# Attention with group normalisation: VectorE's order in slot 0, at the turn of a chunk, and the third chunk's scores over two chunks

## The reference

```
n = groupnorm(x), 32 groups
f = Wq n, g = Wk n (64 x 4096 each), h = Wv n (256 x 4096)
scores[n, m] = sum_q f[q, n] g[q, m]          (4096 x 4096 for each image)
beta = softmax over n of scores
out = x + (gamma * (h beta) + groupnorm(x))
```

## Time and profile before

| | us |
|---|---|
| median of 3 runs | 1918.55 (1916.56 to 1918.79) |
| the profiled execution | 1918.76 |
| its span, first to last instruction | 1917.0 |
| TensorE matmuls busy | 1886.6 |
| VectorE busy | 1631.2 |
| ScalarE busy | 1578.0 |
| GpSimd busy | 1307.8 |

### The profile page before, as it was taken

How to read it: one execution, slowest core, us unless ns; L and a number is a source line. 1 busy time by engine, 2 the same in 40 slices (tenths; PEclk the granted TensorE clock), 3 DMA queues, 4 the chain that set the end, 5 groups by cost and what they waited for, 6 DMA issues and landing times. The chain is left out here.

```text
span 1917.0 us, 44195 instructions
## 1 busy us (share of the span) xinstructions
PE 1886.6 (98%) x17369; PEld 1555.9 (81%) x17369; DVE 1631.2 (85%) x2238; ACT 1578.0 (82%) x1677; POOL 1307.8 (68%) x757
## 2 busy tenths in 40 slices
PE   7899999999999999999999999999999999999999
PEld 4678888877888888887888888888788888888888
DVE  7889998987879999888877999998787788888885
ACT  4788888988768888987877888899787788888885
POOL 4367668876556776886664766788665577767777
PEclk9999999999999999999999999999999999999999
DMA  4022212212102221211211221122121111111111
GB/s 144 4 67 57 67 31 59 66 30 52 44 21 73 75 56 23 76 53 23 70 37 40 53 70 53 37 65 53 29 65 31 22 32 34 24 33 31 33 32 37
DMA packets 200111, 91.19 MB, mean 48 GB/s; under 512 B 150240, under 2 KB 191712, under 8 KB 199904
## 3 DMA queue, kind: packets, MB, share of 16 engines
q1 hardware_dynamic: 199904, 88.36, 17.8%
HBM read 46.60 MB, written 16.78 MB: 33 GB/s over the span
## 5 line engine op out<-in xcount | busy, mean ns | idle before, releaser
L390 POOL TENSOR_TENSOR PL<-SC,PH 128x1024 f16<-128x1024 f32 x511 | 1092.2, 2143 | 549.9 <-ACT SC L643 544.4
L505 PE MATMUL O<-V,PH 128*128 128x257 f16 x4096 | 1119.1, 273 | 0.1
L507 PE MATMUL O<-V,PL 128*128 128x257 f16 x4096 | 1118.8, 273 | 0.0
L506 PE MATMUL O<-V,PH 128*128 128x256 f16 x4096 | 1117.3, 273 | 0.0
L636 ACT ACTIVATE SC<-S 128x1024 f32<-128x1024 f32 x512 | 504.1, 1013 | 136.8 <-issue 122.7
L884 DVE TENSOR_TENSOR SC<-SC,MB 128x1024 f32<-128x1024 f32 x511 | 613.6, 1211 | 0.1
L642 ACT ACTIVATE PH<-SC 128x1024 f16<-128x1024 f32 x511 | 539.4, 1056 | 84.0 <-PE O L507 62.7
L643 ACT ACTIVATE SC<-SC 128x1024 f32<-128x1024 f32 x511 | 532.8, 1043 | 0.0
L841 DVE TENSOR_TENSOR XM<-S,XM 128x1024 f32<-128x1024 f32 x384 | 468.6, 1220 | 74.4 <-PE S L493 64.7
L506 PEld LDWEIGHTS O<-V,PH 128*128 128x128 f16 x4096 | 401.1, 98 | 51.0
L507 PEld LDWEIGHTS O<-V,PL 128*128 128x128 f16 x4096 | 401.1, 98 | 50.1
(11 more groups left out here) (117 smaller groups left out, 1029.4 us busy)
## 6 DMA issues: line engine op xcount, KB each, us to landing
xin<-x SPq DMA_DIRECT2D x24, 1024.0 KB, 5.6
xres<-x SPq DMA_DIRECT2D x64, 256.0 KB, 3.0
ATT<-OT SPq DMA_DIRECT2D x1008, 16.0 KB, 1.8
out<-RES SPq DMA_DIRECT2D x63, 256.0 KB, 2.2
SC<-x SPq DMA_DIRECT2D x8, 512.0 KB, 7.1
F<-GG SPq DMA_DIRECT2D x64, 64.0 KB, 2.0
GG<-GG SPq DMA_DIRECT2D x32, 128.0 KB, 2.4
SC<-wvT SPq DMA_DIRECT2D x1, 256.0 KB, 7.1
```

The source lines that it names most:

```text
L390: pool.tensor_tensor(PL[:, s % RING, :], sc(s), PH[:, s % RING, :], ALU.subtract).then_inc(pl_ready, 1)
L505: mm(o[:, 0:C + 1], PH[:, n % RING, cols], vh, start=t == 0, stop=False)
L506: mm(o[:, 0:C], PH[:, n % RING, cols], vl, start=False, stop=False)
L507: w = mm(o[:, 0:C + 1], PL[:, n % RING, cols], vh, start=False, stop=t == T - 1)
```

## The change

It has three parts.

1. Slot 0. VectorE's maximum(9) moves from between the two halves of slot 0's subtraction to ahead of column_maxima(0). ScalarE's store(9) moves from behind the exponentials of slot 0's first half to ahead of them. (The exchange in the change's name is the sequence of quadrant_maxima, column_maxima and spread_maxima.)
2. The turn of a chunk. Where g is 0 and k is over 0, subtract(n + 4) moves ahead of both maxima of that n. At every other g it stays between them.
3. The third chunk's scores (slots 16 to 23). Before they are made at n = 4, 5, 6 and 7 and the pair 24, 25 at n = 8. After they are made at n = 4, 5, 7 and 8, and the pair 24, 25 at n = 9. turn_maxima(2) moves from n = 7 to n = 8, behind the maxima. exps(6) moves from n = 3 to n = 4, behind store(16) and store(17), and exps(7), exps(8) move one n later; exps(9) stays at n = 6, behind exps(8), and exps(10) stays at n = 7.

```diff
@@ -59,11 +59,11 @@
     NV = 2 * G
 
 
-    SCORES_AT = {1: 12, 2: 14, 4: 16, 5: 18, 6: 20, 7: 22}
-    SCORES_AT.update({n: n + 2 * G for n in range(G, (K - 2) * G, 2)})
+    SCORES_AT = {1: 12, 2: 14, 4: 16, 5: 18, 7: 20, 8: 22, 9: 24}
+    SCORES_AT.update({n: n + 2 * G for n in range(G + 2, (K - 2) * G, 2)})
 
     FIRST_SUB = [(3,), (4, 5), (), (), (8,), (9,), (10,), (11,)]
-    FIRST_EXP = [(), (3,), (4,), (5, 6), (7,), (8,), (9,), (10,)]
+    FIRST_EXP = [(), (3,), (4,), (5,), (6,), (7,), (8, 9), (10,)]
     VU = NFG - 1
     assert len(FG_AT) == NFG and len(V_AT) + len(V_LATE) == NV
 
@@ -684,10 +684,10 @@
                 act.wait_ge(xl_ready[h], NFG)
             store(G)
             round_v(NV - 1, first_v(NV - 1))
+            store(G + 1)
             act.wait_ge(sub_first, 1)
             nc.scalar.activation(PH[:, 0, FIRST], sc(0)[:, FIRST], ACT.Exp, bias=SHIFT)
             nc.scalar.activation(sc(0)[:, FIRST], sc(0)[:, FIRST], ACT.Exp, bias=SHIFT).then_inc(exp_first, 1)
-            store(G + 1)
             act.wait_ge(sub_ready, 1)
             nc.scalar.activation(PH[:, 0, REST], sc(0)[:, REST], ACT.Exp, bias=SHIFT)
             nc.scalar.activation(sc(0)[:, REST], sc(0)[:, REST], ACT.Exp, bias=SHIFT).then_inc(exp_done, 1)
@@ -982,6 +982,7 @@
                     low_v(VU + 2 * i + 1, first_v(VU + 2 * i + 1))
             turn_maxima(0)
             quadrant_maxima(0)
+            maximum(G + 1)
             column_maxima(0)
             spread_maxima(0)
             dve.wait_ge(mb_ready, 1)
@@ -990,8 +991,6 @@
                 half = sc(0)[:, part].rearrange("p (i m) -> p i m", i=GT // 2)
                 ve.tensor_tensor(half, half, MB[:, 0:M].unsqueeze(1).to_broadcast([P, GT // 2, M]),
                                  ALU.subtract).then_inc(done, 1)
-                if part == FIRST:
-                    maximum(G + 1)
             subtract(1)
             low_v(NV - 3, first_v(NV - 3))
             low_v(NV - 2, first_v(NV - 2))
@@ -1007,9 +1006,11 @@
                     divide(k - 1)
                     scale_output(k - 1)
                 q = SCORES_AT.get(n)
+                if g == 0 and k > 0:
+                    subtract(n + SUB_LEAD)
                 if q is not None:
                     maximum(q + 1)
-                if k > 0 and n + SUB_LEAD < K * G:
+                if g > 0 and k > 0 and n + SUB_LEAD < K * G:
                     subtract(n + SUB_LEAD)
                 if q is not None:
                     maximum(q)
@@ -1024,8 +1025,10 @@
                 if k == 0:
                     for s in FIRST_SUB[g]:
                         subtract(s)
-                if g == 7 and k + 2 < K:
+                if g == 7 and 0 < k < K - 2:
                     turn_maxima(k + 2)
+                if n == G:
+                    turn_maxima(2)
                 if g == 1 and k > 0:
                     turn_blocks(k - 1)
                 if g == 1 and 0 < k < K - 1:
```

## The result

The changed kernel takes 1910.28 us (median of 6 runs, 1908.69 to 1911.88), the kernel before 1918.67 in the same runs. The ratio is 0.9957, with a 95% interval of 0.9944 to 0.9970. That is 8.4 us less, where 7.6 were forecast. In a later set of runs the changed kernel took 1911.12 (5 runs) and the kernel before 1918.49: 0.9962, 0.9948 to 0.9975, or 7.4 us less. The profiled execution took 1910.44 us with a span of 1908.7, so 8.3 less than before.

A forecast was written before the change was run, and what follows sets the result against it. TensorE, busy 98% of the span, was taken as the bound, its gaps the whole budget. The start's 2.1 and the turn's 5.5 us sum to 7.6 off 1918.76, giving 1911.2 us; range 1908.4 to 1916.8.

The forecast's parts named there:

- the turn: Subtraction moved into VectorE's idle time before L836 at g = 0; TensorE's waits for maxima and DMAs go, 5.5 us.
- slot 0: At the kernel's start, maximum(9) and store(9) earlier: scores(10) at 67.6, weighing at 72.0, 1.0 us gained by scores(12).
- The third chunk's term: Scores of slots 16 to 23 spread: scores(28) at 122.0 against 123.77; with slot 0 the start gains 2.1 us.
- the start: Everything up to about scores(28), slot 0 and the third chunk's scores together: 2.1 us gained.
- the rest: Gain after the start, from the moved subtraction at the turn of a chunk: 5.5 us.
- The step from the scores to the first half's chain: At slot 0, TensorE's wait before weighing ends with the first half's subtraction, exponentials and low part, at 72.0.
- a fall of the clock: TensorE at 1.2 GHz instead of 2.4 around the scores at 94.05, costing some 1.6 us, expected gone.
- the 0.3 us at scores(28): The pair after scores(28) came 0.27 us late before because VectorE lay behind, and no longer would.
- The first rival: At the start, pauses only move to n = 8 and 9 and the clock drops there too: 1913.3 us, chance 0.2.
- The 12 waits for maxima: In the steady part, TensorE's waits of 0.26 us (9 times) and 0.34 us (3 times) go: 3.3 us.
- The DMA waits: TensorE's three waits that no engine shows, for unit 7's move_f behind regroup in the SP queue: all 2.2 us go.
- The slower rival: At the turn, the subtraction in front delays each of 62 maxima: 1922.7 us, chance 0.04.

The follow-up runs named there:

- moving the DMAs: DMAs moving the next image's f and g of unit 7 issued ahead of the 16 regrouping DMAs: 1914.98 us on the kernel before, 1909.77 us on the changed kernel.

## Why the prediction held, and where it was off

The time (1911.2 against 1910.28) and its range were right, and of the mechanism the turn and slot 0. The third chunk's term was not what it was taken for, and it was small enough not to matter. That the sum came so near is in part luck: by the traces the start gave 1.7 for 2.1 and the rest 6.6 for 5.5, and the interval of the measurement (5.8 to 10.7 us less) couldn't tell 7.6 from either neighbour.

Slot 0: scores(10) at 67.54 (67.6 forecast), weighing at 71.91 (72.0), scores(12) at 76.16 (75.9 to 76.2). The step from the scores to the first half's chain as the thing that ends last is seen: TensorE's wait of 1.70 us before L505 is ended by L418. The 1.0 us is that of one pair of traces; over all fourteen it is 0.7.

Third chunk: scores(18) at 91.78 and their second half at 92.88 (91.8 and 92.85), scores(22) 104.67 (104.6), (24) 110.59 (110.3), (28) 122.38 (122.0). The order of who ends which pause held. The gain at scores(30) was 1.7 and not 2.1. The term that was mis-sized is the third chunk's: 0.7 us from scores(12) to (30) where 1.1 was forecast. maximum(22) ended 0.3 us later than in my schedule. The chain before it was right to 0.06 us (maximum(23) at 107.96 for 107.9), but I took the two maxima as 2.34 us, and they take 2.58 where they follow each other. The pause within scores(26) was 0.67 for 0.55.

Worse than the size is what the term rests on. It counts as gained a fall of the clock that one of five executions didn't have (1.4 us), and the 0.3 us at scores(28), which the turn alone takes away as well. Without these two nothing is left of it: on top of the turn it gained nothing (41.85 us against 41.72 from scores(16) to (30)). Taken alone, the two parts of the start gave 0.9 and 0.5 us by the medians, which the intervals don't tell from nothing. The first rival, the start gives nothing, had chance 0.2; on top of the turn no time measured here rules it out; only slot 0's 0.7 us in the traces speaks against it.

The turn: forecast 5.5, in the traces 6.6 from scores(30) on. Alone on the chip it gave 6.6 too, but that includes the 0.8 at scores(26) and (28), so the two numbers agree by accident (that trace has 7.1 from scores(30) on, and it is the fastest of the five).
- The 12 waits for maxima of 0.26 and 0.34 all went, 3.4 us, for 3.3 forecast.
- Not counted: 12 intervals of 6.88 or 6.89 us instead of 6.79, before the scores at g = 4 of chunks 8 to 11, 1.1 us. I had priced 12 of the 31 waits of the earlier trace rows; 27 are gone from the changed kernel's view. The 0.2 us that is left of the 6.6 is in steps of 0.01.
- The DMA waits gave 1.9 for 2.2. By the distances they were 2.7 before, since the 2.2 that the view shows is a lower bound, and two of the three shrank to 0.64 and 0.20 instead of vanishing. In the first image the transposition came 1.1 us earlier against TensorE, as forecast, but the 16 DMAs behind it took 11.55 us to issue instead of 10.84; in the third 11.12 instead of 10.40. That is 0.7 of the 1.1 each time. Why they took longer stays open, and the waits are not the same in every execution: 0.70, 0 and 0.02 in the second trace of the changed kernel, 0.34, 0 and 0 with the turn alone. That the wait hangs on the place in the queue alone is shown by moving the DMAs: 3.3 us without the change, and no wait left with it.

That the move is free at g = 0 only because it fills idle time was argued there and then tried: at g = 2 the same move costs 2.3 us. That most of its gain comes from the few chunks in which TensorE waits was shown by leaving it out in the 38 other places: 5.6 of 6.6 us stayed.

The slower rival (maxima late at the turn) did not come. In 47 places VectorE still waits for the store of slot 0, so the maximum there is not late at all, and no pair of scores in the steady part waits for one.

## What to carry to other kernels

An engine that is 85% busy can still hold the bound one back for a few tenths in some stages. Count the places where the bound engine waits for it, look for its idle time earlier in the same stage, and put there the work that nobody holds up. In this kernel the advance was worth the sum of those small waits. Before pricing a fall of the clock, look whether a second execution with the same pauses has it. When a change has several parts, try the largest alone before crediting the others: here it gave all that the runs can tell.

## What the runs showed of the hardware

The normalisation L821 on VectorE, a tensor_scalar from SBUF to SBUF, took 0.80 us at its shortest, but 1.26 in this place before and 1.86 in the changed kernel (2.00 with the move at g = 2). The sooner it starts behind GpSimd's L390 (1.41, 0.82 and 0.68 us), the longer it takes. VectorE and GpSimd before:

```profile
316.97 1.26 DVE L821 TENSOR_SCALAR xin<-xin,nmean,nrstd 128x1024 f32<-128x1024 f32 x1
```

```profile
315.56 4.67 POOL L390 TENSOR_TENSOR PL<-SC,PH 128x1024 f16<-128x1024 f32 x2 [1.52 <-ACT SC L643]
```

and after:

```profile
313.77 1.86 DVE L821 TENSOR_SCALAR xin<-xin,nmean,nrstd 128x1024 f32<-128x1024 f32 x1
```

```profile
312.95 4.68 POOL L390 TENSOR_TENSOR PL<-SC,PH 128x1024 f16<-128x1024 f32 x2 [1.35 <-ACT SC L643]
```

The first L390 of the pair, at its mean of 2.14 us, would end at 317.70 before and at 315.09 after, and L821 ends 0.53 and 0.54 us behind that; with the move at g = 2 it is 0.54 again. GpSimd's pair of L390 takes 4.67 us there instead of the 4.23 of pairs elsewhere. So 0.6 of the 1.1 us that the move gained on VectorE was given back in these chunks before the next maximum. The instruction after it in the run with g = 2 as well is the maximum, which stood 0.2 us too late:

```profile
315.49 2.00 DVE L821 TENSOR_SCALAR xin<-xin,nmean,nrstd 128x1024 f32<-128x1024 f32 x1
317.41 1.21 DVE L841 TENSOR_TENSOR XM<-S,XM 128x1024 f32<-128x1024 f32 x1
```

The Trainium skill ("SBUF — State Buffer", section "Who interferes with whom") names tensor_scalar among the instructions that can take the port shared with GpSimd, and says that the one that comes second waits. The rows agree for VectorE: its instruction starts second and ends only behind GpSimd's. Since the 0.53 us behind it are less than the free 0.80, they don't show that it stood still all the while. I had applied the rule to the moved subtraction alone, whose mean stayed at 1.21 us, and not to what moves along with it.
